# State-space scan: products with C one block behind the inputs, constants by transfers, first unit's inputs on VectorE

## The chip, the core and the metric

The program runs on one core of a Trainium2 chip. The time is the device time of one execution in microseconds (us), as a median over runs. The core has a matrix engine (TensorE, PE in the rows; PEld are its weight loads), a vector engine (VectorE, DVE), a scalar engine (ScalarE, ACT), a general engine (GpSimd, POOL) and a sync engine (SyncE, SP) that here only issues transfers. Each engine runs its own instructions in program order and they meet through semaphores.

## What is computed

x has 16 sequences of 512 rows of 256 numbers. It is normalised over its rows to xn; the result is x + A(xn) + F(xn). F is an attention layer and a mixture of experts. A is a state-space layer, and most of the change lies there:

```python
def step(state, inp):                       # for each of 512 time steps
    x_t, dt_t, B_t, C_t = inp
    dA = jnp.exp(jnp.clip(dt_t[:, :, None] * A[None], -10.0, 10.0))
    dB = dt_t[:, :, None] * B_t[:, None, :]
    state = jnp.clip(state * dA + x_t[:, :, None] * dB, -10.0, 10.0)
    y_t = jnp.einsum('bdn,bn->bd', state, C_t) + D * x_t
    return (state, y_t)
...
y = y * _silu(z)
return y @ W_out
```

There are 512 channels d, 16 state numbers n of each channel and 16 sequences b. dt is a softplus of a projection, x_in a SiLU of a convolution over time.

## The kernel before

Three stages run one after the other: build_attn (attention, the shared expert and the routing), build_experts, and build_mamba (the state-space layer with the final sum).

**The state-space stage** works in 32 chunks of 16 time steps. A chunk has four units u = 0 to 3: unit u is sub-chunk s = u // 2 (8 time steps) of half h = u % 2 (256 of the 512 channels, as two blocks i of 128). For each unit:

- POOL (inputs_of, L1530) writes the inputs B·dt·x of the unit into ub[:, h, i], one instruction of 128x2048 for each i, and counts u_ready.
- ACT (decays, L1640) writes the 32 decays exp(-A·dt), 32 instructions.
- DVE (scan, L1734 and L1742) makes 8 steps; a step is a product with the decay (L1734), the product with C of the step before (times_c, L1719), and the clipped sum with the input (L1742). The product with C goes into the same place of ub from which the input of that step was read. The last one of a unit is made in the first step of the next unit, and counts sc_unit.
- PE (nsum, L1884) sums the products over n with 32 matmuls, 16 for each i, and counts nsum_done after each 16.
- DVE (gate_y, L1753) multiplies the sum with the gate, in the seventh step of the next unit.

So ub has one buffer for each half: inputs, then products, then the next inputs of that half. inputs_of waits for nsum_done of the unit two back, for block i = 0 and then for block i = 1.

Between these, POOL makes in a fixed order for each chunk: gate_z of the next chunk (L1515, L1519), inputs of unit 2, dt_sum of the next chunk (L1496, L1502; the second waits for DVE's log_rest L1711, which is made in the first step of unit 2), inputs of unit 3, four gathers of expert rows (L1540), dt_times_x (L1509) of the next chunk, then the inputs of its units 0 and 1. All of it is in one queue. The loop over the chunks has two chunks in its body; the first and the last three stand outside.

SP issues the transfers of a chunk in order: store of the result of the chunk before (L1449), load of the residual (L1436), of the routes, store of B and C, and their loads broadcast over the partitions (L1429, L1431), with the load of rows (L1412) among them. Buffers xm, xn, res, ot, th_z, th_x, sp_u and sp_v each have memory of their own, and dtx has two.

**Ahead of the first chunk** POOL makes dt, dt·x and the inputs of units 0 and 1 in its queue, and DVE starts unit 0 when they are there.

**At the start of the kernel** DVE fills three rows of each of the two tiles kst with ones (L607), then takes the statistics of the first rows (L623, L631), scales w_q (L634) after all 17 weight loads (w_loaded), and makes a reciprocal (L637) on which ACT's first normalisation (L549) waits. ACT and PE each wait for all weight loads ahead of anything else.

## Time and profile before

| | |
|---|---|
| median of 3 runs | 4441.67 us (4422.38 to 4448.53) |
| the profiled execution | 4426.43 us, of which the span of the profile is 4424.3 us |
| state-space stage in the profile | from 2176 us to the end |
| busy, share of the span | PE 85%, DVE 67%, PEld 63%, ACT 57%, POOL 50% |
| busy tenths of DVE, in 40 slices | 4455455544545522222269999999999999999997 |
| busy tenths of POOL, in 40 slices | 2223333333333221000067777777777777777774 |

A slice is 110.6 us. The busy share says how full an engine is; whether it sets the time is seen from its waits. In the rows below a time is the start in us from the start of the span, the number behind it the duration in us, and what stands in brackets is how long the engine stood idle ahead of the instruction and what ended that.

### The profile page before, as it was taken

To read this page: it belongs to the slowest core of one execution; us is meant where nothing else is said; L and a number is where in the kernel's file an instruction comes from. 1 tells how busy PE (TensorE), PEld (TensorE's weight loads), DVE (VectorE), ACT (ScalarE), POOL (GpSimd) and SP (SyncE) were. 2 spreads that over 40 slices of the span, in tenths; PEclk is the share of its full clock that TensorE was granted. 3 is DMA by queue.
4 is the path that set the end of the run, shared out by engine and by line. 5 is a ranking of instruction groups with operands and counts; after the bars stand their busy time and mean duration, and the time that the engine had idled before them with its cause. 6 is when DMAs were issued, how large, how long until landed. Compare 5 with 4: busy or idle time off the path is not lost.

```text
span 4424.3 us, 70363 instructions
## 1 busy us (share of the span) xinstructions
PE 3743.7 (85%) x22136; PEld 2801.6 (63%) x22136; DVE 2973.9 (67%) x5485; ACT 2502.9 (57%) x6473; POOL 2202.6 (50%) x1120
## 2 busy tenths in 40 slices
PE   4888888888888875999869888889898998988886
PEld 2344444444444434777658888878787887888776
DVE  4455455544545522222269999999999999999997
ACT  1443343434433431333378777788778787777773
POOL 2223333333333221000067777777777787777774
PEclk8899999999999987999989999999999999999998
DMA  3322232223322214666522222222222222222221
GB/s 91 95 77 83 84 100 79 78 88 98 91 87 80 79 54 128 212 209 211 150 87 92 76 87 78 80 88 86 78 89 87 75 92 76 87 81 77 87 82 36
DMA packets 285737, 419.86 MB, mean 95 GB/s; under 512 B 77397, under 2 KB 249814, under 8 KB 262808
## 3 DMA queue, kind: packets, MB, share of 16 engines
q1 hardware_dynamic: 273048, 381.12, 26.6%
q0 software_dynamic: 12288, 33.57, 2.2%
q8 instruction: 230, 3.77, 0.4%
q14 instruction: 171, 1.40, 0.1%
HBM read 330.63 MB, written 83.17 MB: 94 GB/s over the span
## 4 chain that ended last, share of the span: by engine, by line
POOL 22%; issue 10%; PE 9%; DVE 8%; ACT 1%; DVEq 0%; POOLq 0%; DMA 0%; SPq 0%; ACTq 0%
POOL m_ub L1530 18%; PE m_Y L1884 7%; DVE m_PR L1734 2%; DVE m_S L1742 2%; DVE m_PR L1742 2%; DVE m_S L1734 1%; POOL m_th_z L1515 1%; POOL m_yg L1540 1%; DVE m_ub L1719 1%; ACT m_dA L1640 1%; POOL m_dtx L1509 1%; PE m_F L1846 1%; PE m_F L1895 0%; PE m_F L1820 0%; DVEq L1733 0%
## 5 line engine op out<-in xcount | busy, mean ns | idle before, releaser
L1530 POOL TENSOR_TENSOR m_ub<-m_Bb,m_dtx 128x2048 f32<-128x2048 f32 x256 | 1157.7, 4546 | 440.4 <-PE m_Y L1884 434.0
L1640 ACT ACTIVATE m_dA<-m_dt,m_a_neg 128x128 f32<-128x128 f32 x4096 | 1211.0, 387 | 168.8 <-DVE m_S L1742 167.6
L1884 PE MATMUL m_Y<-m_ub,m_ident 128*128 128x128 f32 x8192 | 1040.4, 293 | 204.6 <-DVE m_ub L1719 204.6
L1884 PEld LDWEIGHTS m_Y<-m_ub,m_ident 128*128 128x128 f32 x8192 | 1022.1, 208 | 218.4 <-DVE m_ub L1719 218.4
L539 ACT ACTIVATE f_pt<-f_X 128x512 f32<-128x512 f32 (+1 forms) x704 | 371.8, 554 | 712.9 <-PE f_X L841 691.2
L615 DVE TENSOR_REDUCE f_nm<-f_Y 128x1 f32<-128x512 f32 (+3 forms) x896 | 434.1, 530 | 354.4 <-PE f_Y L841 351.4
L1734 DVE SCALAR_TENSOR_TENSOR m_PR<-m_dA,m_S 128x512 f32<-128x512 f32 x512 | 355.6, 695 | 124.5 <-POOL m_ub L1530 53.8
L1734 DVE SCALAR_TENSOR_TENSOR m_S<-m_dA,m_PR 128x512 f32<-128x512 f32 x512 | 354.9, 693 | 12.0
L1742 DVE CUSTOM_DVE_ANT_1 m_PR<-m_PR,m_ub 128x512 f32<-128x512 f32 x512 | 353.2, 690 | 0.2 <-DVE m_PR L1734 0.2
L1742 DVE CUSTOM_DVE_ANT_1 m_S<-m_S,m_ub 128x512 f32<-128x512 f32 x512 | 353.2, 690 | 0.0
L1719 DVE TENSOR_TENSOR m_ub<-m_S,m_Cb 128x512 f32<-128x512 f32 x512 | 349.7, 683 | 0.0
L1719 DVE TENSOR_TENSOR m_ub<-m_PR,m_Cb 128x512 f32<-128x512 f32 x512 | 349.6, 683 | 0.0
L824 PE MATMUL f_Y<-f_kst,f_qst 96*128 96x512 bf16 (+3 forms) x1024 | 254.1, 328 | 107.2 <-DVE f_nm L615 89.7
L830 PE MATMUL f_X<-f_qst,f_kst 99*128 99x512 bf16 (+3 forms) x1024 | 263.0, 324 | 72.7 <-ACT f_pt L539 39.2
L489 POOL TENSOR_TENSOR f_kq<-f_ra,f_rb 128x512 f32<-128x512 f32 x64 | 80.7, 1268 | 459.6 <-DVE f_rb L643 442.6
L1178 DVE SCALAR_TENSOR_TENSOR e_sg<-e_th,e_G 128x512 f32<-128x512 f32 x70 | 48.1, 687 | 326.4 <-ACT e_th L1122 326.4
L1846 PE MATMUL m_F<-m_xpad,m_cv_diag 128*128 128x256 f32 x1024 | 260.3, 398 | 0.0
L824 PEld LDWEIGHTS f_Y<-f_kst,f_qst 96*128 96x128 bf16 x1024 | 84.8, 105 | 260.7 <-DVE f_nm L615 164.2
L1820 PE MATMUL m_F<-m_xnT,m_w_in 128*128 128x256 f32 x1024 | 235.8, 384 | 1.3 <-DMA m_w_in<-L_attn_W_in 1.3
L830 PEld LDWEIGHTS f_X<-f_qst,f_kst 99*128 99x128 bf16 x1024 | 91.5, 103 | 228.0 <-issue 129.4
L1483 POOL MEMSET m_ident<- 128x128 f32 x1 | 0.2, 204 | 470.7 <-POOLq L2012 470.7
L1846 PEld LDWEIGHTS m_F<-m_xpad,m_cv_diag 128*128 128x128 f32 x1024 | 187.2, 193 | 64.6 <-issue 43.6
(229 smaller groups left out, 6278.4 us busy)
## 6 DMA issues: line engine op xcount, KB each, us to landing
m_Bb<-m_bc_dram SPq DMA_DIRECT2D x64, 1024.0 KB, 4.6
m_Cb<-m_bc_dram SPq DMA_DIRECT2D x64, 1024.0 KB, 4.7
f_parts_dram<-f_parts SPq DMA_DIRECT2D x32, 768.0 KB, 4.1
f_kst<-f_parts_dram SPq DMA_DIRECT2D x192, 128.0 KB, 2.6
f_qst<-f_parts_dram SPq DMA_DIRECT2D x192, 128.0 KB, 2.6
e_rows<-sorted_rows SPq DMA_DIRECT2D x70, 256.0 KB, 2.7
e_wg<-Wg SPq DMA_DIRECT2D x70, 256.0 KB, 2.9
e_wu<-Wu SPq DMA_DIRECT2D x70, 256.0 KB, 3.9
```

Of the source, the lines that this page charges most:

```text
L539: act.activation(out, cols(bank_of(k, r)), func, **kw).then_inc(free_sem(k, r), 1)
L615: ins = dve.tensor_reduce(out, cols(full(k, r)), AX.X, ALU.max, negate=True)
L824: pe.matmul(bank[:, c0:c0 + n], qst[p][0:KS, h, qb * P:(qb + 1) * P], kst[p][0:KS, h, 0:n], start=(c0 == 0), stop=False, skip_group_check= ...
L830: pe.matmul(bank[:, c0:c0 + n], kst[p][:, h, kb * P:(kb + 1) * P], qst[p][:, h, kb * P:SEQ], start=(c0 == 0), stop=False, skip_group_check ...
L1530: pool.tensor_tensor(ub[:, h, i, :, :], Bb[:, s, :, :], dtx[:, par, m, None, s * SN:(s + 1) * SN].to_broadcast([P, NST, SN]), ALU.mult).th ...
L1640: last = act.activation(dA[:, h, i, n, :], dtt[:, par, m, s * SN:(s + 1) * SN], ACT.Exp, scale=a_neg[:, m, n:n + 1])
L1719: return dve.tensor_tensor(ub[:, h, :, :, cols], state[:, :].rearrange("p (i n b) -> p i n b", i=2, n=NST), Cb[:, s, None, :, cols].to_bro ...
L1734: dve.scalar_tensor_tensor(new, dA[:, h, :, :, cols].rearrange("p i n b -> p (i n) b"), DA_MIN, old, ALU.max, ALU.mult).then_inc(p_step, 1)
L1742: dve._custom_dve(bass.dve_ops.TENSOR_ADD_SAT, out=new, in0=new, in1=ub[:, h, :, :, cols].rearrange("p i n b -> p (i n) b"), s0=CLIP, s1=- ...
L1820: last = pe.matmul(F[(1 + i) % 4][:, m, :], w_in[:, k, blk * P:(blk + 1) * P], xnT[:, k, :], start=(k == 0), stop=(k == KM - 1))
L1846: last = pe.matmul(F[1 + i][:, j, :], cv_diag[:, k * MI + m, :], xpad[:, m, k * BATCH:k * BATCH + CN], start=False, stop=(k == TAPS - 1))
L1884: last = pe.matmul(Y[:, i * SN:(i + 1) * SN], ident[:, :], ub[:, h, i, n, :], start=False, stop=(n == NST - 1), skip_group_check=True)
```

## The change

In the state-space stage ub gets a third block for each half. The inputs are written into blocks 0 and 1, the products with C into blocks 1 and 2. The inputs of block 0 then wait only for the last step of the scan two units back (s_step); those of block 1 wait for the first 16 matmuls of the sum (nsum_done). dtx has one buffer in place of two, xn lies in xm, ot in res, sp_u in th_z and sp_v in th_x; with that go new waits (dt_ready ahead of ACT's tanh instructions, ot_stored ahead of the load of the residual, xT_done ahead of the load of rows). Ahead of the first chunk DVE makes dt, dt·x and the inputs of unit 0, POOL those of unit 1. At the start of the kernel the ones in kst come by six transfers from a tile of ones, issued by ACT, and ACT and PE wait for the weights only where they first use them.

```diff
@@ -430,6 +430,7 @@
         fixed(pool.memset(ident[:, :], 0.0))
         fixed(pool.affine_select(out=ident[:, :], in_=ident[:, :], compare_op=ALU.not_equal, fill=1.0,
                                  base=0, pattern=[[-1, P]], channel_multiplier=1))
+        fixed(pool.memset(onesb[:, :], 1.0))
         for q, value in enumerate((-0.5, 0.5, 1e-5, -1.0)):
             fixed(pool.memset(consts[:, q, :], value))
 
@@ -446,7 +447,6 @@
             fixed(pool.memset(before[:, :, :], 0.0))
             fixed(pool.affine_select(out=before[:, :, :], in_=before[:, :, :], compare_op=ALU.is_ge, fill=1.0,
                                      base=0, pattern=[[-1, ER], [1, ER]], channel_multiplier=0))
-            fixed(pool.memset(onesb[:, :], 1.0))
             fixed(pool.memset(tri[:, :], 0.0))
             fixed(pool.affine_select(out=tri[:, :], in_=tri[:, :], compare_op=ALU.is_ge, fill=1.0,
                                      base=0, pattern=[[-1, P]], channel_multiplier=1))
@@ -527,11 +527,15 @@
         run(nc.gpsimd, do)
         pool.wait_ge(scattered, 16 * TT * TOPK * BATCH)
 
-    N_CONST, N_CONST_FIRST = 26, 6
+    N_CONST, N_CONST_FIRST = 26, 7
 
     @block.scalar
     def _(act):
-        act.wait_ge(w_loaded, W_ALL)
+        act.wait_ge(const_ready, N_CONST_FIRST)
+        for p in range(2):
+            for q in range(PARTS):
+                act.dma_start(kst[p][KS + q:KS + q + 1, :, :].rearrange("a h t -> a (h t)").rearrange("a (p c) -> a p c", p=P),
+                              onesb[:, 0:NH * SEQ // P]).then_inc(q_scaled, 16)
 
         def reader(r):
             def read(k, out, cols, func, **kw):
@@ -562,6 +566,8 @@
                     last = act.activation(h2[:, t, :], x2[:, t, :], ACT.Copy, scale=sc2[:, 4, t:t + 1])
                 last.then_inc(h2_done, 1)
             if kind == "T":
+                if isinstance(b, int) and b == 0:
+                    act.wait_ge(w_loaded, W_ALL)
                 for k in range(KM):
                     read(("T", k), h1T[:, k, :], lambda bank: bank[:, :], ACT.Copy, scale=ln1[:, k:k + 1])
             if kind == "lat":
@@ -603,9 +609,6 @@
 
     @block.vector
     def _(dve):
-        for p in range(2):
-            dve.memset(kst[p][KS:KS + PARTS, :, :], 1.0).then_inc(q_scaled, 1)
-
         def full(k, r):
             dve.wait_ge(*filled(k, r))
             return bank_of(k, r)
@@ -758,7 +761,6 @@
 
     @block.tensor
     def _(pe):
-        pe.wait_ge(w_loaded, W_ALL)
         pe.wait_ge(const_ready, N_CONST_FIRST)
 
 
@@ -782,6 +784,8 @@
                 pe.wait_ge(h1_done, b + 1)
                 transposed("T", r, h1)
             if kind == "lat":
+                if isinstance(b, int) and b == 0:
+                    pe.wait_ge(w_loaded, W_ALL)
                 pe.wait_ge(*used(("T", 0), r))
                 pe.wait_ge(*used(("T", 1), r))
                 pe.sem_inc(taken)
@@ -791,7 +795,7 @@
                 full(("lat",), r, last)
             if kind == "kq":
                 if isinstance(b, int) and b == 0:
-                    pe.wait_ge(q_scaled, 3)
+                    pe.wait_ge(q_scaled, 1 + 16 * 2 * PARTS)
                 g, first, second = i, ("kq", i, j, 0), ("kq", i, j, 1)
                 if j == 0:
                     pe.wait_ge(*used(("lat",), r))
@@ -1273,7 +1277,7 @@
 
     xm = sb("m_xm", [P, TT, DM])
     rowsc = sb("m_rowsc", [P, TT, 2])
-    xn = sb("m_xn", [P, TT, DM])
+    xn = xm
     xnT = sb("m_xnT", [P, KM, CN])
     xpad = sb("m_xpad", [P, MI, HALO + CN])
     th_z = sb("m_th_z", [P, MI, CN])
@@ -1281,23 +1285,23 @@
     dt_in = sb("m_dt_in", [RANK + 1, CN])
     bc_row = sb("m_bc_row", [RANK + 2 * NST, CN])
     sp_e = sb("m_sp_e", [P, MI, CN])
-    sp_u = sb("m_sp_u", [P, MI, CN])
-    sp_v = sb("m_sp_v", [P, MI, CN])
+    sp_u = th_z
+    sp_v = th_x
     sp_r = sb("m_sp_r", [P, MI, CN])
     z_sb = sp_r
 
     x2 = sb("m_x2", [P, 2, MI, CN])
     zs = sb("m_zs", [P, 2, MI, CN])
     dtt = sb("m_dt", [P, 2, MI, CN])
-    dtx = sb("m_dtx", [P, 2, MI, CN])
+    dtx = sb("m_dtx", [P, MI, CN])
 
     dA = sb("m_dA", [P, 2, 2, NST, SN])
-    ub = sb("m_ub", [P, 2, 2, NST, SN])
+    ub = sb("m_ub", [P, 2, 3, NST, SN])
     Bb = sb("m_Bb", [P, NSUB, NST, SN])
     Cb = sb("m_Cb", [P, NSUB, NST, SN])
     yz = sb("m_yz", [P, MI, CN])
     res = sb("m_res", [P, TT, DM])
-    ot = sb("m_ot", [P, TT, DM])
+    ot = res
     info = sb("m_info", [P, 2, TT, 2 * TOPK])
     info_i = info[:, :, :, :].bitcast(mybir.dt.int32)
     yg = sb("m_yg", [P, TOPK, TT, DM])
@@ -1408,7 +1412,7 @@
 
         def load_x(c):
             rows = row_of(c)
-            held(xn_done, TT * c)
+            held(xT_done, c)
             sp.dma_start(xm[:, :, :], x_tm[bass.ds(rows, CN), :].rearrange("(j p) d -> p j d", p=P)).then_inc(x_loaded, 16)
             with nc.allow_non_contiguous_dma(reason="two numbers of a row"):
                 sp.dma_start(rowsc[:, :, :], stat_tm[bass.ds(rows, CN), :].rearrange("(j p) d -> p j d", p=P)).then_inc(x_loaded, 16)
@@ -1432,7 +1436,7 @@
 
         def load_res(c):
             rows = row_of(c)
-            held(ot_done, c)
+            held(ot_stored, 16 * c)
             sp.dma_start(res[:, :, :], res_tm[bass.ds(rows, CN), :].rearrange("(j p) d -> p j d", p=P)).then_inc(res_loaded, 16)
 
         def load_info(c, par):
@@ -1504,9 +1508,8 @@
         def dt_times_x(c, par):
             pool.wait_ge(dt_ready, c + 1)
             pool.wait_ge(x2_ready, 2 * (c + 1))
-            if not isinstance(c, int) or c >= 2:
-                pool.wait_ge(u_ready[NU - 1], 2 * (c - 1))
-            pool.tensor_tensor(dtx[:, par, :, :], x2[:, par, :, :], dtt[:, par, :, :], ALU.mult).then_inc(dtx_ready, 1)
+            pool.wait_ge(u_ready[NU - 1], 2 * c)
+            pool.tensor_tensor(dtx[:, :, :], x2[:, par, :, :], dtt[:, par, :, :], ALU.mult).then_inc(dtx_ready, 1)
 
         def gate_z(c, par):
 
@@ -1526,9 +1529,12 @@
             for i in range(2):
                 m = 2 * h + i
                 if not isinstance(pc, int) or pc >= 1:
-                    pool.wait_ge(nsum_done[pu], 2 * (pc - 1) + i + 1)
+                    if i == 0:
+                        pool.wait_ge(s_step, NU * ST * (pc - 1) + ST * (pu + 1) + 2)
+                    else:
+                        pool.wait_ge(nsum_done[pu], 2 * (pc - 1) + 1)
                 pool.tensor_tensor(ub[:, h, i, :, :], Bb[:, s, :, :],
-                                   dtx[:, par, m, None, s * SN:(s + 1) * SN].to_broadcast([P, NST, SN]),
+                                   dtx[:, m, None, s * SN:(s + 1) * SN].to_broadcast([P, NST, SN]),
                                    ALU.mult).then_inc(u_ready[u], 1)
 
         def gather(c, par):
@@ -1541,9 +1547,6 @@
                                             bass.IndirectOffsetOnAxis(ap=info_i[:, par, j, k:k + 1], axis=0)).then_inc(yg_loaded, 16)
 
         gate_z(0, 0)
-        dt_sum(0, 0)
-        dt_times_x(0, 0)
-        inputs_of(0, 0, 0)
         inputs_of(0, 0, 1)
 
         def body(c, par, first, last):
@@ -1591,6 +1594,7 @@
                 act.activation(xpad[:, 2 * hx:2 * hx + 2, HALO:HALO + CN], F[1 + hx][:, :, :], ACT.Copy).then_inc(xpad_ready, 1)
                 act.wait_ge(xz_done, 4 * c + 2 * i + 2)
                 act.wait_ge(zs_ready, c)
+                act.wait_ge(dt_ready, c)
                 act.activation(th_z[:, 2 * i:2 * i + 2, :], F[(3 + i) % 4][:, :, :], ACT.Tanh, scale=0.5).then_inc(thz_ready, 1)
                 act.wait_ge(sp_sub, c)
                 act.activation(z_sb[:, 2 * i:2 * i + 2, :], F[(3 + i) % 4][:, :, :], ACT.Copy).then_inc(z_copied, 1)
@@ -1600,6 +1604,7 @@
                 hx = 1 - i
                 act.wait_ge(conv_done, 2 * c + i + 1)
                 act.wait_ge(x2_ready, 2 * c)
+                act.wait_ge(dt_ready, c)
                 act.activation(th_x[:, 2 * hx:2 * hx + 2, :], F[1 + hx][:, :, :], ACT.Tanh, scale=0.5).then_inc(thx_ready, 1)
 
         def evac_dbc(c):
@@ -1716,7 +1721,7 @@
             s, h = u // 2, u % 2
             cols = slice(t * BATCH, (t + 1) * BATCH)
             state = (S[h], PR)[(t + 1) % 2]
-            return dve.tensor_tensor(ub[:, h, :, :, cols], state[:, :].rearrange("p (i n b) -> p i n b", i=2, n=NST),
+            return dve.tensor_tensor(ub[:, h, 1:3, :, cols], state[:, :].rearrange("p (i n b) -> p i n b", i=2, n=NST),
                                      Cb[:, s, None, :, cols].to_broadcast([P, 2, NST, BATCH]), ALU.mult)
 
         def scan(c, u, between, before_it):
@@ -1740,7 +1745,7 @@
                 dve.wait_ge(p_step, base + t + 1)
                 dve.sem_inc(taken)
                 dve._custom_dve(bass.dve_ops.TENSOR_ADD_SAT, out=new, in0=new,
-                                in1=ub[:, h, :, :, cols].rearrange("p i n b -> p (i n) b"),
+                                in1=ub[:, h, 0:2, :, cols].rearrange("p i n b -> p (i n) b"),
                                 s0=CLIP, s1=-CLIP).then_inc(s_step, 1)
                 if t in between:
                     between[t]()
@@ -1778,6 +1783,20 @@
         dve.tensor_scalar(a_neg[:, :, :], a_neg[:, :, :], -1.0, None, ALU.mult).then_inc(setup_neg, 1)
         silu_x(0, 0)
         log_rest(0)
+        dve.wait_ge(sp_ln, 1)
+        dve.wait_ge(sp_relu, 2)
+        dve.tensor_tensor(sp_u[:, :, :], sp_u[:, :, :], sp_r[:, :, :], ALU.add).then_inc(sp_sub, 1)
+        dve.wait_ge(sp_sub, 1)
+        dve.wait_ge(sp_low, 1)
+        dve.tensor_tensor(dtt[:, 0, :, :], sp_u[:, :, :], sp_v[:, :, :], ALU.subtract).then_inc(dt_ready, 1)
+        dve.wait_ge(dt_ready, 1)
+        dve.wait_ge(x2_ready, 2)
+        dve.tensor_tensor(dtx[:, :, :], x2[:, 0, :, :], dtt[:, 0, :, :], ALU.mult).then_inc(dtx_ready, 1)
+        dve.wait_ge(dtx_ready, 1)
+        dve.wait_ge(b_loaded[0], 16)
+        for i in range(2):
+            dve.tensor_tensor(ub[:, 0, i, :, :], Bb[:, 0, :, :], dtx[:, i, None, 0:SN].to_broadcast([P, NST, SN]),
+                              ALU.mult).then_inc(u_ready[0], 1)
 
         def body(c, par, first, last):
             slots = [dict() for _ in range(NU)]
@@ -1881,7 +1900,7 @@
             pe.wait_ge(sc_unit[u], c + 1)
             for i in range(2):
                 for n in range(NST):
-                    last = pe.matmul(Y[:, i * SN:(i + 1) * SN], ident[:, :], ub[:, h, i, n, :], start=False, stop=(n == NST - 1),
+                    last = pe.matmul(Y[:, i * SN:(i + 1) * SN], ident[:, :], ub[:, h, 1 + i, n, :], start=False, stop=(n == NST - 1),
                                      skip_group_check=True)
                 last.then_inc(nsum_done[u], 1)
 
```

## Rows read from the trace of the kernel before

**Rows 1.** Groups of VectorE, 2311 to 4200 us: busy us, mean ns | idle before, releasers.

```profile
L1734 DVE SCALAR_TENSOR_TENSOR m_PR<-m_dA,m_S 128x512 f32<-128x512 f32 x447 | 310.4, 695 | 82.2 <-issue 30.2 <-DVE m_S L1742 28.3 <-POOL m_ub L1530 13.7
...
L1753 DVE TENSOR_TENSOR m_yz<-m_Y,m_zs 128x256 f32<-128x256 f32 x112 | 46.2, 413 | 0.0
```

**Rows 2.** Timeline of VectorE, first steps of units following each other.

```profile
3117.84 0.70 DVE L1734 SCALAR_TENSOR_TENSOR m_PR<-m_dA,m_S 128x512 f32<-128x512 f32 x1 [2.49 <-issue]
...
3134.40 0.70 DVE L1734 SCALAR_TENSOR_TENSOR m_PR<-m_dA,m_S 128x512 f32<-128x512 f32 x1
...
3151.35 0.70 DVE L1734 SCALAR_TENSOR_TENSOR m_PR<-m_dA,m_S 128x512 f32<-128x512 f32 x1 [0.89 <-DVE m_S L1742]
...
3168.04 0.70 DVE L1734 SCALAR_TENSOR_TENSOR m_PR<-m_dA,m_S 128x512 f32<-128x512 f32 x1
...
3184.14 0.69 DVE L1734 SCALAR_TENSOR_TENSOR m_PR<-m_dA,m_S 128x512 f32<-128x512 f32 x1 [0.51 <-POOL m_ub L1530]
```

**Rows 3.** Timeline of GpSimd in the same chunk.

```profile
3124.82 9.04 POOL L1530 TENSOR_TENSOR m_ub<-m_Bb,m_dtx 128x2048 f32<-128x2048 f32 x2 [9.16 <-PE m_Y L1884]
...
3142.11 9.05 POOL L1530 TENSOR_TENSOR m_ub<-m_Bb,m_dtx 128x2048 f32<-128x2048 f32 x2 [3.39 <-PE m_Y L1884]
...
3154.56 2.36 POOL L1502 TENSOR_TENSOR m_dt<-m_sp_u,m_sp_v 128x1024 f32<-128x1024 f32 x1 [1.08 <-issue]
...
3158.33 9.05 POOL L1530 TENSOR_TENSOR m_ub<-m_Bb,m_dtx 128x2048 f32<-128x2048 f32 x2 [1.41 <-PE m_Y L1884]
...
3167.53 0.99 POOL L1540 DMA_INDIRECT m_yg<-expert_rows,m_info  x1
...
3174.90 9.03 POOL L1530 TENSOR_TENSOR m_ub<-m_Bb,m_dtx 128x2048 f32<-128x2048 f32 x2 [0.22 <-POOL m_dtx L1509]
```

**Rows 4.** Timeline of TensorE in the same chunk.

```profile
3119.19 9.04 PE L1884 MATMUL m_Y<-m_ub,m_ident 128*128 128x128 f32 x64 [4.06 <-DVE m_ub L1719]
...
3152.69 9.04 PE L1884 MATMUL m_Y<-m_ub,m_ident 128*128 128x128 f32 x64 [3.18 <-DVE m_ub L1719]
```

**Rows 5.** Timeline ahead of the first chunk, ScalarE and GpSimd.

```profile
2219.14 1.28 ACT L1640 ACT_TABLE_LOAD   x1 [4.92 <-POOL m_dt L1502]
...
2220.43 18.81 ACT L1640 ACTIVATE m_dA<-m_dt,m_a_neg 128x128 f32<-128x128 f32 x64
...
2221.56 17.95 POOL L1530 TENSOR_TENSOR m_ub<-m_Bb,m_dtx 128x2048 f32<-128x2048 f32 x4
```

**Rows 6.** Timeline of VectorE in the first chunk.

```profile
2230.64 0.70 DVE L1734 SCALAR_TENSOR_TENSOR m_PR<-m_dA,m_S 128x512 f32<-128x512 f32 x1 [17.91 <-POOL m_ub L1530]
...
2272.37 1.29 DVE L1711 SCALAR_TENSOR_TENSOR m_sp_v<-m_F,m_sp_e 128x512 f32<-128x512 f32 x2 [2.35 <-ACT m_F L1623]
...
2309.62 0.70 DVE L1734 SCALAR_TENSOR_TENSOR m_PR<-m_dA,m_S 128x512 f32<-128x512 f32 x1 [3.89 <-POOL m_ub L1530]
```

**Rows 7.** Timeline of GpSimd at the end of the loop.

```profile
4189.11 0.95 POOL L1540 DMA_INDIRECT m_yg<-expert_rows,m_info  x1 [5.68 <-issue]
```

**Rows 8.** Timeline of VectorE at the end of the loop.

```profile
4204.27 0.69 DVE L1734 SCALAR_TENSOR_TENSOR m_PR<-m_dA,m_S 128x512 f32<-128x512 f32 x1 [5.71 <-POOL m_ub L1530]
```

**Rows 9.** Groups of VectorE, 4205 us to the end.

```profile
L1734 DVE SCALAR_TENSOR_TENSOR m_PR<-m_dA,m_S 128x512 f32<-128x512 f32 x47 | 32.6, 695 | 8.9 <-POOL m_ub L1530 7.3
```

**Rows 10.** Timeline of VectorE at the start of the kernel.

```profile
11.06 6.88 DVE L607 MEMSET f_kst<- 3x8192 bf16 x1 [1.66 <-issue]
...
23.33 0.18 DVE L637 RECIPROCAL f_sc<-f_sc 128x4 f32<-128x4 f32 x1 [3.16 <-POOL f_sc L473]
```

**Rows 11.** Transfers, 0 to 60 us: busy tenths in 40 slices; packets, MB, engine share.

```profile
DMA  0599879998000000000000000000000000680675
...
q1 hardware_dynamic: 5513, 5.00, 28.6%
```

**Rows 12.** Timeline in the attention stage, VectorE and GpSimd.

```profile
769.18 0.22 DVE L722 TENSOR_TENSOR f_picked<-f_oh,f_wt 128x56 f32<-128x56 f32 x1
...
781.34 1.09 DVE L734 TENSOR_TENSOR f_picked<-f_oh,f_slot 128x56 f32<-128x56 f32 x1
...
781.09 1.27 POOL L489 TENSOR_TENSOR f_kq<-f_ra,f_rb 128x512 f32<-128x512 f32 x1 [2.20 <-DVE f_rb L643]
```

## The prediction

> **What bounds the kernel now.** The slices of the page say that VectorE is nine tenths busy from the second fifth of the state-space stage to its end, and no other engine is; so the question for that stage is what VectorE's remaining idle time waits for. I read the groups of VectorE first. In the loop over the chunks all idle time of note stands ahead of L1734, the first step of a unit [rows 1]: 30.2 us under "issue", 28.3 us under "DVE m_S L1742" and 13.7 us under "POOL m_ub". The first is the jump back at the end of the loop body, one of about 2.3 us in each two chunks, as in the 2.49 us of [rows 2]; nothing in the change touches it. The second is named after VectorE itself, but that engine had long been done. The timeline shows who it was: the inputs that begin at 3142.11 end at 3151.16, and unit 2 starts at 3151.35; those that begin at 3174.90 end at 3183.93, and the next chunk starts at 3184.14 [rows 2, 3]. Both labels are therefore one wait, for GpSimd's inputs, and together 42.0 us.
>
> Why GpSimd is late is read from its own idle time: 9.16, 3.39 and 1.41 us ahead of its inputs, each ended by TensorE's sum L1884 [rows 3]. GpSimd may write over a buffer only after TensorE has summed the products in it, and both blocks (9.05 us) stand behind that. The cycle is: last product, 16 matmuls, two input instructions, next unit of that half.
>
> **Part 1: a third block (loop).** After the change the input of block 0 needs only the end of the scan two units back, that of block 1 the first half of the sum. I set the chunk of [rows 2 to 4] again, with U0 to U3 as the starts of its units. VectorE's own work takes 16.5 us for unit 0 (3117.84 to 3134.4), 16.7 for unit 2 and 15.6 for unit 3 [rows 2], 16.05 for unit 1.
> - Unit 2: block 0 can be written from U0 + 16.6 to 21.1. The half sum is there at 3142.11, U0 + 24.3, so block 1 is ready at U0 + 28.8, where unit 2 is due at U0 + 32.55. It was ready at 33.3. The 0.9 us go, with 3.7 us to spare.
> - Unit 1: the half sum is there at 3124.82, U0 + 7.0; block 1 is ready at U0 + 11.5, due at 16.5.
> - Unit 3: dt ends at 3156.92, U2 + 5.6 [rows 3], and it isn't moved, since it hangs on VectorE's log_rest in unit 2. Then 9.05 us of inputs with no wait between them: 3152.69 starts the sum, 3158.33 has half of it [rows 3, 4], and block 1 needs it only at U2 + 10.1. Ready at U2 + 14.6, due at U2 + 16.7.
> - Unit 0 of the next chunk: four gathers and dt·x take 3167.53 to 3174.90, 7.4 us, then 9.03 us [rows 3]. From U2 + 14.8 that ends at U2 + 31.2; due at U2 + 16.7 + 15.6 = 32.3. This is the tightest place, with 1.1 us to spare.
>
> So all waits for inputs in the loop fall away, **42.0 us**. What is late next is nothing within a unit: VectorE is then bound by its own steps and the jumps. GpSimd's reordered instructions are the same ones at the same price; it runs beside the same steps as before, only earlier.
>
> **Part 2: the end of the loop and the last chunks.** At the loop's end one gather is held up by 5.68 us [rows 7], on no semaphore that the profile shows, and VectorE waits 5.71 us at 4204.27 [rows 8]. That delay stays. The inputs of unit 3 end 1.3 us earlier there (by the same sum: from dt without the 1.4 us wait for TensorE), so **1.3 us**; with luck up to 3.4, what is left above a jump of 2.3. Behind that, 7.3 us of waits for inputs [rows 9] go as in the loop: **7.3 us**. The very end (last sum, gate, projection) isn't touched.
>
> **Part 3: ahead of the first chunk.** VectorE's 256-wide product takes 413 ns and a 512-wide one about 695 [rows 1], so some 1.1 ns an element: an estimate of 1.27 us for 1024 elements and 2.4 for 2048. GpSimd's two instructions for dt kept ScalarE waiting 4.92 us [rows 5]; two of VectorE take 2.6 with the hops between. dt is ready 2.2 us earlier, at about 2216.9. dt·x (1.3) and two inputs (4.8) would be done at about 2223, but the decays of unit 0 take a table load of 1.28 and half of 18.81 us [rows 5]: 2227.6. So unit 0 starts 3.0 us earlier than at 2230.64 [rows 6], not 7. In its first chunk VectorE then waits for ScalarE at log_rest (2272.37, [rows 6]), which moves by the 2.2 us of dt only; the waits ahead of it melt into that one. From there 2.2 us remain, and the 3.89 us ahead of the next chunk [rows 6] go as in the loop: **6.1 us**.
>
> VectorE's new instructions have both operands in SBUF, and GpSimd's inputs of unit 1 start on the same signal. The trace shows what that does: a small product of two such operands takes 0.22 us alone, but 1.09 us where it starts at 781.34 beside a GpSimd instruction that ends at 782.36; it ends as that one does [rows 12]. So VectorE's inputs may stand behind GpSimd's, 4.5 + 2.4 + 4.5 + 2.4 us from 2218.2, and unit 0 starts at 2232 in place of 2227.6. The wait at log_rest hides this too, so the 6.1 us stand; were that cover gone, it would cost 4.4 us. The Trainium skill says in "SBUF — State Buffer", section "Who interferes with whom", that a DVE instruction with two SBUF inputs contends with a GpSimd instruction that reads SBUF, and that whoever issues first holds the shared ports for all of it. By that rule, the trace agrees for the first unit; and in the loop each instruction of VectorE has one operand in PSUM, so the rule has nothing to take there. If it did bind in the loop, the gain of part 1 would be in doubt; it is what speaks most against moving work between these two engines.
>
> **Part 4: the start of the kernel.** Two fills of 6.88 us stand ahead of the statistics on VectorE; the second ends at 17.9, and the reciprocal on which all waits runs at 23.33 [rows 10]. Without them it waits for the weights, since the scaling of w_q stands ahead of it. All transfers are over by the tenth slice of 1.5 us, 15.0 us [rows 11]; with their signal and the scaling the reciprocal could run at about 15.9. The six transfers of ones add 768 short packets. From 28.6% of 16 engines over 60 us for 5513 packets [rows 11], a packet costs 50 ns of one engine, so 768 cost 2.4 us over 16 engines if all were full, nothing if they fit in gaps. The reciprocal comes at 15.9 to 18.3; I take 17.1, **6.2 us** less (5.0 to 7.4). The work of the attention stage follows from that instruction in a chain, so it moves as a whole. ScalarE issues the six ahead of its first normalisation, by about 6 us, long before it is due; TensorE's wait for the ones lies at its first kq, past 25 us.
>
> **Part 5: shared memory and new waits**, all costed at nothing.
> - ScalarE waits for dt_ready ahead of the tanh of z. dt is ready at U2 + 5.6; ScalarE gets there after the decays of unit 3, 9.4 us and a table load into unit 2, at about U2 + 11.5. Behind it in its queue are the decays of the next chunk, which wait for U3 anyway. Cover: 5.9 us.
> - SP waits for the result to be stored before it loads the residual, some 3 us longer. Behind it stand the routes and the loads of B and C. The load of C waits for unit 1 anyhow, and B is wanted at U2 + 22, some 20 us later than it lands.
> - dtx with one buffer: dt·x already stands behind the inputs of unit 3 in GpSimd's queue. The load of rows waits for a transpose made a unit before.
>
> **The sum**: 42.0 + 1.3 + 7.3 + 6.1 + 6.2 = 62.9 us. The profiled execution took 4426.43 us, so 4363.5. The median of the runs shown is 15 us above that execution; taken off it, 4441.67 - 62.9 = **4378.8 us**.
>
> **The rivals.**
> - *The slack isn't there* (18%). The tightest place has 1.1 us in 66, worked out from one chunk, and GpSimd's spans are rough. If the chain from dt over the gathers to the next inputs is longer by that, half of the 49.3 us stays as waits: 62.9 - 24.7 = 38.2 us, 4403.5. For it: GpSimd still has some 53 us of work in 66. Against: its durations hardly vary.
> - *TensorE takes over* (8%). It is the busiest engine over the span, 85%. If its sums set the starts, through the gate or the blocks of ub, none of parts 1 and 2 is had: 12.3 us, 4429.4. Against: it waits 4.06 and 3.18 us for VectorE at its sums [rows 4], so it follows VectorE and not the other way round.
> - *Slower* (4%): dt_ready comes late. The tanh of z now waits for dt, which stands in GpSimd's queue behind the inputs of unit 2 and behind VectorE's log_rest. If GpSimd makes dt more than 5.9 us later than now, ScalarE stands; it hurts VectorE only once the decays of the next chunk come late too, which take 9.4 of the 15.6 us of unit 3, so from 5.9 + 6.2, some 12 us later than now. Each us beyond costs 31 us in 31 chunks; 3 us beyond would give 4441.7 - 62.9 + 93 = 4472.
>
> **Chances.** The forecast 70%, the rivals 18, 8 and 4%. About 0.5% (22 us) is what a measurement of this kernel can tell from no change. Faster: 70 + 18 = 0.88; same: 0.08; slower: 0.04. The range takes in the forecast's own spread and the first rival. Low: 4360, from the sum off the profiled time and 3 us more of bounds (2.1 at the loop's end, 1.2 at the start). High: 4406, the first rival with the start's bound.
>
> **What the profile would show.** Ahead of L1734 the labels "DVE m_S" and "POOL m_ub" shrink to near nothing in the loop, "issue" stays at 30 us. GpSimd's two inputs of a unit stand apart, the first right after a unit's end, the second behind L1884. The first unit starts at 2228 or 2232 less the 6 us of the start, the reciprocal near 17. Wrong would be: POOL waits that stay ahead of unit 0 (the slack), waits of the gate L1753 for TensorE, or decays L1640 that end late.

## The result, and the profile after

| | median | runs |
|---|---|---|
| kernel before | 4443.73 us | 4 runs, 4422.38 to 4448.53 |
| changed kernel | 4381.06 us | 4 runs, 4378.37 to 4389.52 |

The ratio is 0.9881 with a 95% interval of 0.9853 to 0.9909: 53 us less, between 40 and 65. The medians of the table are 62.7 us apart, and in a second set of runs (below) the changed kernel took 4394.23 us beside 4437.29 for before, 43.1 apart, ratio 0.9894. The forecast was 4378.8 us. That closeness is partly luck: the saving worked out was 62.9 us, counted from waits in the profiled execution of before. The profiled execution of the changed kernel took 4378.37 us with a span of 4376.6, so between the two profiles only **47.7 us** went, and the rest came from a median of before that lies above its profiled execution. It is the 47.7 that have to be accounted for.

The page of the changed kernel, busy time of TensorE and VectorE's tenths in 40 slices:

```profile
PE 3733.1 (85%) x22136; PEld 2784.6 (64%) x22136; DVE 2974.2 (68%) x5488; ACT 2499.8 (57%) x6473; POOL 2194.1 (50%) x1115
...
DVE  3455455544545432222279999999999999999998
```

VectorE is nine tenths busy to the end of the state-space stage, as before. Its groups in the loop (2299 to 4160 us), first step of the pair and first clipped sum:

```profile
L1739 DVE SCALAR_TENSOR_TENSOR m_PR<-m_dA,m_S 128x512 f32<-128x512 f32 x447 | 310.4, 694 | 42.4 <-issue 30.5
...
L1747 DVE CUSTOM_DVE_ANT_1 m_PR<-m_PR,m_ub 128x512 f32<-128x512 f32 x448 | 309.3, 690 | 10.0 <-issue 10.0
```

The first row answers [rows 1]: 82.2 us have become 42.4, "DVE m_S" and "POOL m_ub" are no longer among its releasers, and "issue" stands at 30.5. The second row is new: 10.0 us of "issue" ahead of a clipped sum, which had none before. The timeline of VectorE over one pair of chunks shows where:

```profile
3095.62 0.70 DVE L1739 SCALAR_TENSOR_TENSOR m_PR<-m_dA,m_S 128x512 f32<-128x512 f32 x1 [2.31 <-issue]
...
3096.22 0.68 DVE L1724 TENSOR_TENSOR m_ub<-m_S,m_Cb 128x512 f32<-128x512 f32 x1
...
3097.58 0.70 DVE L1747 CUSTOM_DVE_ANT_1 m_PR<-m_PR,m_ub 128x512 f32<-128x512 f32 x1 [0.68 <-issue]
...
3112.94 0.69 DVE L1739 SCALAR_TENSOR_TENSOR m_PR<-m_dA,m_S 128x512 f32<-128x512 f32 x1
...
3129.03 0.69 DVE L1739 SCALAR_TENSOR_TENSOR m_PR<-m_dA,m_S 128x512 f32<-128x512 f32 x1
...
3145.72 0.70 DVE L1739 SCALAR_TENSOR_TENSOR m_PR<-m_dA,m_S 128x512 f32<-128x512 f32 x1
...
3161.35 0.70 DVE L1739 SCALAR_TENSOR_TENSOR m_PR<-m_dA,m_S 128x512 f32<-128x512 f32 x1
```

The units at 3112.94, 3129.03, 3145.72 and 3161.35 start with no wait. The jump is there as before (2.31), and two instructions behind it the clipped sum waits another 0.68 us for nothing that the profile names. GpSimd in the same chunk:

```profile
3112.99 4.55 POOL L1536 TENSOR_TENSOR m_ub<-m_Bb,m_dtx 128x2048 f32<-128x2048 f32 x1 [1.25 <-DVE m_S L1747]
...
3120.70 4.55 POOL L1536 TENSOR_TENSOR m_ub<-m_Bb,m_dtx 128x2048 f32<-128x2048 f32 x1 [3.15 <-PE m_Y L1903]
...
3134.58 9.08 POOL L1536 TENSOR_TENSOR m_ub<-m_Bb,m_dtx 128x2048 f32<-128x2048 f32 x2
...
3151.19 9.05 POOL L1536 TENSOR_TENSOR m_ub<-m_Bb,m_dtx 128x2048 f32<-128x2048 f32 x2 [0.24 <-POOL m_dtx L1512]
```

These rows answer [rows 3]. For unit 2 the two blocks stand apart: the first at 3112.99, right after a scan's end (3112.94 is the next unit's first step), the second at 3120.70 behind TensorE's sum. Unit 3's 9.08 us stand together with no wait. The next chunk's, at the place that had 1.1 us to spare on paper, end at 3160.24, and VectorE starts at 3161.35: 1.1 us.

To see where the 47.7 us lie, I cut each span at fixed instructions: the end of attention (VectorE's first instruction of the expert stage), the start of the state-space stage (GpSimd's first m_ident), the first step of chunks 0, 1 and 29, and the end.

| us | before | after | less | forecast |
|---|---|---|---|---|
| attention stage | 1705.0 | 1702.4 | 2.6 | 6.2 |
| expert stage | 470.7 | 467.9 | 2.8 | 0 |
| state space, up to the first unit | 55.0 | 51.9 | 3.1 | 3.0 |
| chunk 0 | 79.0 | 75.3 | 3.7 | 3.1 |
| loop, chunk 1 to chunk 29, with its end | 1894.7 | 1864.7 | 30.0 | 43.3 |
| last chunks and end | 220.0 | 214.4 | 5.6 | 7.3 |

### The profile page after: what moved, and what is told of

The parts are those of the page before. It is cut to its first block, busy times and chain, and to the rows that moved or that the text cites. A ratio compares the mean times of both kernels' runs of the same rounds, so it can differ in the third digit from the quotient of the medians.

```text
span 4376.6 us, 70452 instructions
## 1 busy us (share of the span) xinstructions
PE 3733.1 (85%) x22136; PEld 2784.6 (64%) x22136; DVE 2974.2 (68%) x5488; ACT 2499.8 (57%) x6473; POOL 2194.1 (50%) x1115
## 4 chain that ended last, share of the span: by engine, by line
DVE 35%; issue 11%; PE 2%; ACT 1%; DVEq 1%; POOL 0%; DMA 0%; SPq 0%; POOLq 0%; ACTq 0%
DVE m_S L1747 8%; DVE m_PR L1747 8%; DVE m_S L1739 7%; DVE m_PR L1739 7%; DVE m_ub L1724 1%; DVE m_yz L1758 1%; ACT m_dA L1645 1%; DVE m_x L1708 1%; DVE m_th_x L1716 1%; DVEq L1738 1%; PE m_F L1865 1%; DVE m_res L1766 0%; PE m_Y L1903 0%; POOL m_ub L1536 0%; PE m_F L1839 0%
## 5 line engine op out<-in xcount | busy, mean ns | idle before, releaser
L1903 PE MATMUL m_Y<-m_ub,m_ident 128*128 128x128 f32 x8192 | 1024.9, 290 | 161.4 <-DVE m_ub L1724 161.4
L1903 PEld LDWEIGHTS m_Y<-m_ub,m_ident 128*128 128x128 f32 x8192 | 1007.3, 206 | 174.2 <-DVE m_ub L1724 174.2
L1739 DVE SCALAR_TENSOR_TENSOR m_PR<-m_dA,m_S 128x512 f32<-128x512 f32 x512 | 355.5, 694 | 53.6 <-issue 30.5
L1487 POOL MEMSET m_ident<- 128x128 f32 x1 | 0.2, 205 | 467.9 <-POOLq L2031 467.9
L1865 PEld LDWEIGHTS m_F<-m_xpad,m_cv_diag 128*128 128x128 f32 x1024 | 186.5, 192 | 63.9 <-issue 43.1
```

The source lines that it names most:

```text
L1739: dve.scalar_tensor_tensor(new, dA[:, h, :, :, cols].rearrange("p i n b -> p (i n) b"), DA_MIN, old, ALU.max, ALU.mult).then_inc(p_step, 1)
L1865: last = pe.matmul(F[1 + i][:, j, :], cv_diag[:, k * MI + m, :], xpad[:, m, k * BATCH:k * BATCH + CN], start=False, stop=(k == TAPS - 1))
L1903: last = pe.matmul(Y[:, i * SN:(i + 1) * SN], ident[:, :], ub[:, h, 1 + i, n, :], start=False, stop=(n == NST - 1), skip_group_check=True)
```

## The experiments

The state-space stage is the sharper measure: its length repeats within 1 to 3 us for the same kernel (2206.3 in the profile of the changed kernel, 2209.3 in another, below). The 3 us lie in chunk 0, which took 75.3 us in the one and 78.4 in the other. There TensorE's convolution products took nearly twice as long for a while (the second group of them, after and then the other profile), and VectorE waited 2.54 us for TensorE's sum at a gate where it had waited 0.46, and 0.86 for ScalarE behind it:

```profile
2237.55 1.99 PE L1865 MATMUL m_F<-m_xpad,m_cv_diag 128*128 128x256 f32 x8
```

```profile
2253.95 3.78 PE L1865 MATMUL m_F<-m_xpad,m_cv_diag 128*128 128x256 f32 x8
```

The granted clock over chunk 0 is 0.81 in the one and 0.78 in the other. The loop repeats within 1 us (1864.7 and 1865.5). The attention stage does not repeat: nearly the same instructions took 1697 to 1739 us in the profiles of this study, so each comparison below is by stage where the trace allows it. The next three kernels ran on one chip, beside runs of before with a median of 4431.38 us.

**Each part alone: the start.** The changed kernel with the old start: the two fills on VectorE, and the early waits for the weights.

```diff
-                act.dma_start(kst[p][KS + q:KS + q + 1, :, :]..., onesb[:, 0:NH * SEQ // P]).then_inc(q_scaled, 16)
+        act.wait_ge(w_loaded, W_ALL)
...
+            dve.memset(kst[p][KS:KS + PARTS, :, :], 1.0).then_inc(q_scaled, 1)
...
+        pe.wait_ge(w_loaded, W_ALL)
```

> The changed kernel with only the start of the kernel as it was before: ones in kst by two fills on VectorE, ScalarE and TensorE wait for all weights first. My theory: the new start is worth the 2.5 us by which the attention stage ends earlier in the profile of the changed kernel (2.6 us at the first product with the rope table), not the 4.8 us of the reciprocal and not the 6.2 forecast, because TensorE runs the first products at the lower clock after it. So 2 to 3 us slower than the changed kernel, some 50 us faster than the kernel before. Rival: the 2.8 us by which the experts' stage came out shorter belong to it too; then 5 us slower. On the gap of 0.76 us behind the jump of the loop: if it comes from where the loop lies in VectorE's instructions, it may change here, since two fills are added ahead.

Median 4390.0 us (4 runs, 4376.75 to 4419.12), ratio to before 0.989 (0.9862 to 0.9918). The runs spread over 42 us and can't tell 2 us from 5. The profile can: reciprocal at 23.34, first product of the rotation (L645 after) at 40.85 us, where the changed kernel has it at 35.59. Over the profiles of this study, nine with the new start have it at 33.4 to 36.2, mean 34.6; three with the old one have it at 38.2, 38.2 and 40.85, mean 39.1. The start is worth some 4.5 to 4.8 us, not 6.2. The new start, ScalarE's queue and VectorE:

```profile
2.42 4.04 ACTq L537 DMA_DIRECT2D f_kst<-f_onesb  x6
...
4.77 1.40 DVE L626 BATCH_NORM_STATS2 f_st<-f_xm 128x6 f32<-128x256 f32 x4 [4.77 <-DMA f_xm<-x_tm]
...
18.10 0.42 DVE L637 TENSOR_SCALAR f_w_q<-f_w_q 64x512 f32<-64x512 f32 x1 [11.60 <-DMA f_ln<-w_ln]
...
18.56 0.18 DVE L640 RECIPROCAL f_sc<-f_sc 128x4 f32<-128x4 f32 x1
...
35.59 0.69 DVE L645 TENSOR_TENSOR f_ra<-f_Z,f_rope 128x512 f32<-128x512 f32 x1 [16.85 <-PE f_Z L807]
```

The reciprocal is at 18.56 and not at 17.1: the scaling ahead of it waits for the last of the weights to 18.10. That load's signal came at 15.9 in before (issued at 10.15, landed 5.7 us later) and at 18.1 here (issued at 11.51, landed 6.6 us later), although the six transfers carry 16 KB each. Behind the reciprocal the two profiles differ too. From TensorE's first transpose to that product it is 12.7 us after and 10.1 before, since two of the three groups of products between them took nearly twice as long. After, then before:

```profile
25.83 3.75 PE L794 MATMUL f_Z<-f_h1T,f_w_lat 128*128 128x512 f32 x4 [0.98 <-ACT f_h1T L543]
...
30.32 2.04 PE L805 MATMUL f_Z<-f_lat,f_w_q 64*128 64x512 f32 x2 [0.73 <-issue]
...
32.29 3.26 PE L807 MATMUL f_Z<-f_h1T,f_w_kra 128*128 128x512 f32 x4
```

```profile
30.89 3.52 PE L790 MATMUL f_Z<-f_h1T,f_w_lat 128*128 128x512 f32 x4 [0.82 <-ACT f_h1T L539]
...
35.15 1.09 PE L801 MATMUL f_Z<-f_lat,f_w_q 64*128 64x512 f32 x2 [0.73 <-issue]
...
36.17 1.98 PE L803 MATMUL f_Z<-f_h1T,f_w_kra 128*128 128x512 f32 x4
```

That is TensorE's clock, and not the new start's doing. The view of the clock reads 1.00 in these stretches only because the trace has no record there: the first one, at the full level, stands at 34.9 us in this profile of the changed kernel and at 34.1 in that of before. In every profile of the study a product of 512 columns takes 1.06 us ahead of that first record and 0.59 us behind it, so it marks the rise. The rise came 12 to 15 us after TensorE's first instruction in some executions and 6 to 7 in others. With it the time from the reciprocal to the product L645 is 17.0 to 17.6 us or 14.6 to 14.9, under either start: long in this kernel and in four of the nine with the new start, the changed kernel's profile among them; short in the other five, in before and in the kernel before with twelve counts (below). So the lower clock that was put down above is there, but it doesn't take back what the new start gains: the two profiles under Result happened to be one of each kind.

**Each part alone: the first unit.** dt, dt·x and the inputs of the first unit back on GpSimd, with the third block and the new start kept.

```diff
+        dt_sum(0, 0)
+        dt_times_x(0, 0)
+        inputs_of(0, 0, 0)
         inputs_of(0, 0, 1)
...
-        dve.tensor_tensor(sp_u[:, :, :], sp_u[:, :, :], sp_r[:, :, :], ALU.add).then_inc(sp_sub, 1)
...
-            dve.tensor_tensor(ub[:, 0, i, :, :], Bb[:, 0, :, :], dtx[:, i, None, 0:SN].to_broadcast([P, NST, SN]),
```

> The changed kernel with dt, dt*x and the inputs of unit 0 of the first chunk on GpSimd again. My theory: unit 0 starts 3 us later against the start of the stage, and 2.2 us of that last to the next chunk; so 2 to 3 us slower than the changed kernel. Rival A (ports shared by VectorE and GpSimd): VectorE's two-operand products stood behind GpSimd's in the changed kernel, so putting them back costs under 1 us. Rival B: the 0.76 us at the first clipped sum behind each jump (10 us in 13 jumps) comes from the dozen instructions that stand ahead of VectorE's loop; without them the gap goes, and this kernel is 7 us faster than the changed one.

Median 4382.47 us (4371.72 to 4389.04), ratio 0.9878 (0.9849 to 0.9907). By stages the first unit comes 2.3 us later than in the changed kernel (54.2 us into the stage against 51.9), chunk 1 only 1.0 us later (128.2 against 127.2), and yet the state-space stage is **10.3 us shorter** (2196.0): the loop takes 1854.0 where the changed kernel takes 1864.7. Its groups, in the loop:

```profile
L1742 DVE SCALAR_TENSOR_TENSOR m_PR<-m_dA,m_S 128x512 f32<-128x512 f32 x447 | 310.4, 694 | 42.4 <-issue 30.5
...
L1750 DVE CUSTOM_DVE_ANT_1 m_PR<-m_PR,m_ub 128x512 f32<-128x512 f32 x448 | 309.1, 690 | 0.0
```

The 10.0 us ahead of the clipped sum are gone, with an identical loop: the lines are three further down, and the instructions and their waits are the same. Only what stands ahead of the loop in VectorE's queue differs. So the work moved to VectorE brings 2.3 us at the first unit, of which 1.0 is left at chunk 1, and costs 10 in the loop. Rival B was right. In the changed kernel the inputs themselves show the two engines in each other's way. VectorE, then GpSimd:

```profile
2212.62 8.81 DVE L1798 TENSOR_TENSOR m_ub<-m_Bb,m_dtx 128x2048 f32<-128x2048 f32 x2
...
2222.20 0.70 DVE L1739 SCALAR_TENSOR_TENSOR m_PR<-m_dA,m_S 128x512 f32<-128x512 f32 x1 [0.77 <-ACT m_dA L1645]
...
2263.53 1.29 DVE L1716 SCALAR_TENSOR_TENSOR m_th_x<-m_F,m_sp_e 128x512 f32<-128x512 f32 x2 [6.00 <-ACT m_F L1628]
...
2212.67 13.14 POOL L1536 TENSOR_TENSOR m_ub<-m_Bb,m_dtx 128x2048 f32<-128x2048 f32 x2 [19.74 <-DVE m_dtx L1794]
```

VectorE's two inputs take 8.81 us, where two alone would take 4.8 by the estimate of part 3, and GpSimd's two take 13.14 in place of 9.04 [rows 3]. Both start at 2212.6 and take turns, VectorE first: the four instructions end at 2214.91, 2219.28, 2221.43 and 2225.81, VectorE's and GpSimd's in turn. [rows 12] had shown the like for a small one. The prediction had priced GpSimd's going first, which would have put VectorE's second input 4.5 us later. The Trainium skill says in "SBUF — State Buffer", section "Who interferes with whom", that a VectorE instruction with two SBUF inputs contends with a GpSimd instruction that reads SBUF; by that rule, the trace agrees. It cost nothing here: unit 0 waits 0.77 us for the decays at the end, and what is left melts into the wait of 6.00 us at 2263.53 for ScalarE (2.35 in [rows 6]), as the sum had it.

**The earlier waits, taken away.** Both blocks wait for the sum as before, in the changed kernel; the third block's memory stays.

```diff
-                    if i == 0:
-                        pool.wait_ge(s_step, NU * ST * (pc - 1) + ST * (pu + 1) + 2)
-                    else:
-                        pool.wait_ge(nsum_done[pu], 2 * (pc - 1) + 1)
+                    pool.wait_ge(nsum_done[pu], 2 * (pc - 1) + i + 1)
```

> The changed kernel, three blocks and shared buffers kept, but the input of block 0 waits for TensorE's sum as in the kernel before. My theory: the earlier start of block 0 is the whole gain in the state-space stage; the waits ahead of L1739 come back in the loop (some 40 us) and behind it (5 to 7 us), so 40 to 47 us slower than the changed kernel, and within 12 us of the kernel before. Rival: part of the gain comes from the shared buffers or from the earlier first unit, which shift the engines against each other; then less than 30 us slower than the changed kernel.

Median 4436.21 us (10 runs), ratio to before 1.001 (0.9991 to 1.003): with the old waits put back (block 0 for the first half of the sum, block 1 for the second) nothing is left of the whole change that these runs can tell. The state-space stage takes 2262.4 us, 56.1 more than in the changed kernel: 46.5 more in the loop, 5.5 behind it, 4 ahead of it. The group of the first steps in the loop, over the same steps as [rows 1]:

```profile
L1736 DVE SCALAR_TENSOR_TENSOR m_PR<-m_dA,m_S 128x512 f32<-128x512 f32 x447 | 310.3, 694 | 88.1 <-DVE m_S L1744 34.9 <-issue 30.4 <-POOL m_ub L1533 12.8
```

The waits for GpSimd are 47.7 us against 42.0 in [rows 1], and "issue" is as it was. What makes the 5.7 us more was not tried; the waits on the sum are before's word for word, so it lies in something else that the change brought. The gap behind the jump (9.2 us here) is still in it, so the loop is 16.5 us longer than before's. That the earlier start of the inputs is the gain in the loop is shown; how much of it is block 0's wait and how much block 1's was not tried apart.

**Where the slack ends.** The first rival rested on 1.1 us of slack. Two kernels put a piece of dt·x once more into GpSimd's queue, ahead of the product in dt_times_x: one block of four (0.8 us in a chunk) or all four (2.5 us, 2.6 in what was expected), each with a wait for it.

```diff
+            pool.tensor_tensor(dtx[:, 0:1, :], x2[:, par, 0:1, :], dtt[:, par, 0:1, :], ALU.mult).then_inc(filled_up, 1)
+            pool.wait_ge(filled_up, c)
```

> The changed kernel with one more product of 256 numbers on GpSimd in each chunk, ahead of dt*x (about 0.8 us with its hop), in the chain from dt over the gathers to the inputs of the next chunk. My theory: the chain has 1.1 us to spare (in the profile of the changed kernel the inputs end at 3160.24 and the next chunk starts at 3161.35), so the state-space stage keeps its 2206 us within 3. Rival: GpSimd already sets the start of unit 0; then 0.8 us a chunk, 25 us more.

> As the one with 256 numbers, but 1024 (a second dt*x, 2.4 us and 0.2 of hop). My theory: 2.6 us less the 1.1 to spare is 1.5 us in each chunk whose end isn't a jump of the loop, and less where a jump gives 2.3 us more: some 25 to 30 us more in the state-space stage (2232 to 2236), as waits ahead of unit 0 for GpSimd. Rival A: GpSimd sets the pace, 2.6 us in each chunk, 80 us. Rival B: TensorE sets it, under 10 us.

Each was executed once: 4396.23 and 4414.64 us, beside 4446.21 for before. With 0.8 us the state-space stage took 2207.0 us and the loop 1865.0, as without it. With 2.5 us they took 2232.5 and 1887.3, 22.6 us more in the loop. Its group over the loop, then a first step behind a jump and the next one with no jump ahead:

```profile
L1742 DVE SCALAR_TENSOR_TENSOR m_PR<-m_dA,m_S 128x512 f32<-128x512 f32 x447 | 310.4, 694 | 62.8 <-POOL m_ub L1539 46.6 <-issue 4.8
```

```profile
3116.54 0.70 DVE L1742 SCALAR_TENSOR_TENSOR m_PR<-m_dA,m_S 128x512 f32<-128x512 f32 x1 [2.38 <-issue]
...
3183.93 0.70 DVE L1742 SCALAR_TENSOR_TENSOR m_PR<-m_dA,m_S 128x512 f32<-128x512 f32 x1 [1.55 <-POOL m_ub L1539]
```

A chunk that begins behind a jump waits some 2.3 us as ever; most of these now stand under GpSimd's name and not under "issue", since the late inputs fall within the jump. What is new is the 1.5 us at each of the 14 chunks of the loop that begin without a jump: the idle time ahead of the first steps is 20.4 us more (62.8 against 42.4), and the wait at the loop's end 2.5 more. So 2.5 us on GpSimd came through as 1.5: the slack is there, some 1.0 us, and the 1.1 us fit.

**The gap behind the jump.** Two explanations stood: the new kernel's loop holds something that stalls the clipped sum, or the place of the loop in VectorE's instruction stream does it. The second can be moved without touching the loop: instructions that only count a semaphore, ahead of it. Twelve of them in the kernel **before**, and 32 in the changed kernel:

```diff
+        for _ in range(12):          # 32 in the changed kernel
+            dve.sem_inc(taken)
         silu_x(0, 0)
```

> The kernel before with twelve instructions that only count a semaphore on VectorE, ahead of its loop over the chunks; nothing else. Theory of place: the gap of 0.76 us at the first clipped sum behind each jump in the changed kernel comes from where the loop lies in VectorE's instructions, since eleven more (thirteen instructions with waits, less two fills) stand ahead of it. Then the gap shows here too, 0.7 to 1.1 us in each of 13 jumps, and the loop gets some 10 us longer, or less where a wait for inputs swallows it. Rival: the gap belongs to the three blocks or the shared buffers; then none here, and the stage keeps its 2249 us.

> The changed kernel with 32 instructions that only count a semaphore on VectorE ahead of its loop. Theory of place: the gap of 0.76 us behind each jump is a matter of where the loop starts, so it moves or goes; if it goes, the state-space stage takes 10 us less, near 2196 us as in the run with the first unit on GpSimd. Rival: the first unit on VectorE causes it in another way; then the gap stays and the stage takes 2206 us.

Each was executed once. The kernel before with twelve counts took 4464.01 us (beside 4446.21 without them), and its state-space stage was 21.2 us longer (2269.9; the loop 1913.6, 18.9 more). The jump itself has doubled: the last sum of the body ends at 3143.97, and the next step follows 4.33 us later.

```profile
3143.28 0.69 DVE L1742 CUSTOM_DVE_ANT_1 m_S<-m_S,m_ub 128x512 f32<-128x512 f32 x1
...
3148.30 0.70 DVE L1734 SCALAR_TENSOR_TENSOR m_PR<-m_dA,m_S 128x512 f32<-128x512 f32 x1 [4.33 <-issue]
```

Over the loop "issue" is 57.1 us in place of 30.2, and the waits for inputs went down from 42.0 to 33.6, since GpSimd works on through the longer jump. The gap at the clipped sum that was expected did not show: at its new place this loop pays at the jump itself. In the changed kernel 32 counts took the gap away: stage 2194.1, loop 1853.4. This one execution took 4360.59 us, 17.8 less than the profiled one of the changed kernel; 5.2 us of that are the attention stage.

To see what that is worth in runs, the changed kernel and the one with the counts ran again on one chip, beside before at 4437.29 us.

> The changed kernel again, beside the three that follow. My theory: the state-space stage takes 2206 us within 2 in every execution; what differs between executions of one kernel is the attention stage (1697 to 1739 us from profile to profile so far, with TensorE's mean clock from 0.923 to 0.936). So the profile shows 2204 to 2208 us in that stage, and the median lies 45 to 60 us under the kernel before. Rival: the state-space stage itself varies by 10 us, and the gains read from single profiles aren't what the change is worth.

> The changed kernel with 32 instructions on VectorE ahead of the loop that only count a semaphore. My theory: the loop loses the gap behind each jump, 11 to 12 us, in every execution; median 8 to 14 us below that of the changed kernel. Rival: the one profile was a lucky one; within 4 us of the changed kernel.

The changed kernel: 4394.23 us (4382.79 to 4397.28), ratio 0.9894 (0.9859 to 0.993), stage 2209.3, loop 1865.5. With the counts: 4381.2 us (4372.85 to 4384.51), ratio 0.9867 (0.9833 to 0.9901), stage 2196.1, loop 1853.5. By stages it is 12 to 13 us, twice; the medians differ by 13.0 and their ranges overlap. VectorE behind a jump, with the counts:

```profile
3109.54 0.70 DVE L1739 SCALAR_TENSOR_TENSOR m_PR<-m_dA,m_S 128x512 f32<-128x512 f32 x1 [2.26 <-issue]
...
3110.14 0.68 DVE L1724 TENSOR_TENSOR m_ub<-m_S,m_Cb 128x512 f32<-128x512 f32 x1
...
3110.75 0.69 DVE L1747 CUSTOM_DVE_ANT_1 m_PR<-m_PR,m_ub 128x512 f32<-128x512 f32 x1
```

The jump takes 2.26 us as ever, and the clipped sum at 3110.75 follows at once. The other kernels agree: those that have the changed kernel's instructions ahead of the loop all have the gap, whatever GpSimd does beside it (9.2 us with the wait for the sum, 9.6 and 9.8 with the two fillers), and the one with the old start, two instructions further on, has 12.2. Why the place matters, and at which places it does, isn't settled: three positions are known with no gap (before, the first unit on GpSimd, 32 counts), two with one, and one with a doubled jump.

**A still earlier start.** If the reciprocal waits for weights that it doesn't need, the wait can be taken from it. The column loads go first, under a signal of their own, and the scaling of w_q goes behind the first reciprocal; the 32 counts are kept.

```diff
+            sp.dma_start(ln1[:, :], w_ln1.rearrange("(k p) -> p k", p=P)).then_inc(lns_loaded, 16)
...
-                    act.wait_ge(w_loaded, W_ALL)
+                    act.wait_ge(lns_loaded, 32)
...
+                if isinstance(b, int) and b == 0:
+                    dve.wait_ge(w_loaded, W_ALL)
+                    dve.tensor_scalar(w_q[LAT:P, :, :, :], w_q[LAT:P, :, :, :], 1.0 / math.sqrt(HD), None, ALU.mult).then_inc(q_scaled, 1)
```

> The 32 instructions, and the start of the kernel once more: the two small column loads go first and have a semaphore of their own, VectorE scales w_q after the first reciprocal, so that only TensorE's first product with a weight waits for the 15 weight loads. My theory: the reciprocal runs near 10 us in place of 18.6, the transposes follow, and the latent product starts when the weights are there, near 17 us in place of 25.8; the first product with the rope table at 26 to 29 us (33.4 to 36.1 so far), so the attention stage starts 7 us earlier. Rival: TensorE's clock takes most of it back, as with the first step of this kind (4.8 us at the reciprocal, some 2.6 to 4.4 left at the rope product); then 3 us or less.

The chain at the start, VectorE and then TensorE:

```profile
9.83 0.18 DVE L638 RECIPROCAL f_sc<-f_sc 128x4 f32<-128x4 f32 x1 [3.46 <-POOL f_sc L474]
...
28.08 0.69 DVE L646 TENSOR_TENSOR f_ra<-f_Z,f_rope 128x512 f32<-128x512 f32 x1 [9.35 <-PE f_Z L808]
...
14.46 1.94 PE L779 MATMUL f_Z<-f_ident,f_h 128*128 128x128 f32 x8 [14.46 <-POOL f_run L455]
...
18.42 3.75 PE L795 MATMUL f_Z<-f_h1T,f_w_lat 128*128 128x512 f32 x4 [2.02 <-DMA f_wd<-Wd]
...
22.91 2.04 PE L806 MATMUL f_Z<-f_lat,f_w_q 64*128 64x512 f32 x2 [0.73 <-issue]
```

The reciprocal is at 9.83 us. Of the 8.7 us gained there some 7 are left at the product L646 (28.08 here, 26.12 in the last kernel below, against a mean of 34.6), as TensorE's first product waits at 18.42 for the weights after all. Median 4372.19 us (4365.52 to 4379.06), ratio 0.9856 (0.982 to 0.9892). The ranges of this kernel and of the one with the counts alone (4372.85 to 4384.51) overlap, so in runs the second new start isn't told apart.

**Fewer jumps.** Four chunks in a loop body, so 6 jumps back in place of 13; with the 32 counts.

```diff
-            with eng.Fori(0, NCH // 2 - 2) as g:
-                body(g * 2 + 1, 1, False, False)
-                body(g * 2 + 2, 0, False, False)
+            with eng.Fori(0, (NCH - 4) // 4) as g:
+                body(g * 4 + 1, 1, False, False)
...
+                body(g * 4 + 4, 0, False, False)
```

> The 32 instructions, and four chunks in the body of the loop in place of two, on every engine. My theory: 6 jumps of VectorE in place of 13, each 2.3 us, so 16 us less in the loop (1837 from 1853), if the longer body brings no stalls of its own. Rival: the longer body must be fetched in pieces and stalls in its middle, on VectorE or on TensorE with some 1300 instructions in it; then the gain is under 5 us, or a loss.

Median 4363.14 us (4351.83 to 4368.1), ratio 0.9831 (0.9794 to 0.9869). The loop takes 1837.5 us, 16.0 less than with two chunks in a body; "issue" ahead of the first steps is 14.0 us in place of 30. Seven jumps at 2.3 us are 16.1. The jump's price is shown by this, and the longer body brings no stall of its own.

**All together.** The start, the counts and four chunks in a body.

> The 32 instructions, four chunks in the loop body and the second new start in one kernel. My theory: the parts lie in different stages and add up: state-space stage 2180 to 2184 us, the first rope product near 28 us; median 5 to 9 us below the kernel with four chunks and the 32 instructions alone, some 78 us below the kernel before. Rival: the new start's gain is lost in the attention stage, whose length differs by up to 40 us between executions; then it can't be told from that kernel.

Median 4356.2 us (6 runs, 4340.14 to 4364.23), beside before at 4430.13 on that chip: ratio 0.982 (0.9789 to 0.985), state-space stage 2178.6 us. It is the fastest kernel of this study, 74 us under before; by the ratios (0.982 against 0.9881 and 0.9894) it is some 27 to 33 us under the changed kernel.

**The attention stage.** What makes its length vary isn't settled. Stretch, length, busy time of PE, PEld, DVE, ACT and POOL with instructions, then the granted clock, the DMA share and GB/s, for 60 to 1700 us; the kernel before, the changed one, the one with the old start, and the one with 32 counts:

```profile
60.00:1700.00 1640.00, 1358.49 (x7720) 696.92 (x7720) 786.90 (x1919) 641.64 (x1189) 520.58 (x510) 0.91 0.27 83
```

```profile
60.00:1700.00 1640.00, 1363.30 (x7720) 697.05 (x7720) 787.23 (x1919) 640.79 (x1189) 520.58 (x510) 0.91 0.27 83
```

```profile
60.00:1700.00 1640.00, 1374.23 (x7659) 703.65 (x7659) 778.06 (x1890) 638.27 (x1180) 512.12 (x499) 0.89 0.27 83
```

```profile
60.00:1700.00 1640.00, 1356.62 (x7718) 690.74 (x7716) 790.12 (x1928) 640.72 (x1189) 523.25 (x524) 0.91 0.27 83
```

The work is the same, its matmuls longer or shorter in sum (1356.6 to 1374.2 us for nearly as many), and the granted clock is 0.89 in the longest of the four and 0.91 in the others. The profile with the old start had 1738.6 us in that stage, the one with 32 counts 1697.2, and neither kernel changes anything there beyond the first 40 us. The profile of before ran with the same clock as that of after, so this doesn't explain the missing gain; but it is why I read the start's worth at the product L645 and not at the end of the stage.

## Why the prediction was right, and where it was off

**Right:** the reading of two labels as one wait. With the earlier waits both are gone in the loop, and putting the old ones back costs 46.5 us there. The other ways that I had named did not come: the slack of 1.1 us is measured as 1.0 (0.8 us more on GpSimd costs nothing, 2.5 come through as 1.5 a chunk), VectorE waits for TensorE nowhere in the loop, and no wait for dt_ready shows up. The last chunks gained 5.6 us (forecast 7.3), the end of the loop waits 4.34 us in place of 5.71 [rows 8], 1.4 against a forecast of 1.3:

```profile
4162.25 0.70 DVE L1739 SCALAR_TENSOR_TENSOR m_PR<-m_dA,m_S 128x512 f32<-128x512 f32 x1 [4.34 <-POOL m_ub L1536]
```

**Right, but in part not told apart:** part 3. The first unit came 3.1 us earlier (3.0), the two engines took turns, and the wait for ScalarE at log_rest covered it. The first chunk's share in all was 6.8 us (6.1) in this profile, but 4.1 in the second one of the same kernel (chunk 0 took 78.4 us in place of 75.3). And of the 6.8 us, 5.8 were there with the first unit's inputs on GpSimd too, where the sum had given the blocks 3.9: for the move itself, priced at 2.2 by chunk 1, 1.0 is left, less than chunk 0 varies by.

**Off, part 1.** "42.0 us" was the sum of the waits, and "nothing in the change touches it" was said of the jump. The waits did go, and the idle time ahead of the first steps fell by 39.8 us; a wait that goes still leaves the ordinary 0.03 us between two units. Then the sentence on the jump failed: the change puts ten-odd instructions ahead of the loop in VectorE's queue, and with the loop at that place each jump is followed by another 0.7 us at the clipped sum, 10.0 us in all. The loop with its end gave 30.0 us in place of 43.3. That the place does it is shown from three sides: fewer instructions ahead (10.7 us back in the loop), 32 more (11.3 and 12.0 back), and the kernel before with twelve more (18.9 us lost, though at the jump itself and not at the clipped sum). I had priced part 3 by the time of its instructions and its ports, and had no term for what an instruction ahead of a loop does to the loop.

**Off, part 4.** The term was 6.2 us (5.0 to 7.4); the reciprocal came 4.8 us earlier, at 18.56 where 15.9 to 18.3 was forecast and 17.1 taken. Two sizes of the sum were off. The six transfers had been costed by their packets at 0 to 2.4 us and taken at 1.2; the signal of the last weights came 2.2 us later, at 18.1 against 15.9. And 0.9 us had been allowed for that signal and the scaling behind the last transfer at 15.0; they take 1.3, since the signal alone comes at 15.9. The chain behind moves as forecast, but has one of two lengths, some 2.5 us apart, by when TensorE's clock rises, whichever the start: the profile of before had the short one, that of the changed kernel the long one, and so only 2.6 us show in the table.

**What was not foreseen at all** is the expert stage, 2.8 us shorter with no change in it; over the profiles it lies between 467.5 and 473.4 us, so that is its spread.

The sum of these: 39.8 - 10.0 + 1.4 is 31.2 us for the loop and its end by idle time; by the cut it is 30.0, since VectorE's own steps took 1.3 us more in all (1797.5 against 1796.2). With 6.8 for the first chunk, 5.6 for the last, 2.6 and 2.8 ahead of the stage it is 47.7 us, but for rounding. The medians are 62.7 us apart all the same, because before's stands 17.3 us over its profiled execution and after's 2.7: those 14.6 us stood in for the 15.2 that the sum had too much. That the forecast time came out within 2.3 us of the median is luck; that the saving was forecast with the right mechanism, and too large by a quarter of itself, is not.

## What to carry to other kernels

Follow a wait to the engine that was really late, and give its cycle one more buffer only where a dependence other than the last one can release it: here the next inputs need the scan's end, not the sum of all its products, and taking that away again cost 46 us in the loop. Before work is moved onto the engine that bounds a loop, count what stands ahead of the loop in its queue, and compare "issue" at and behind the jump by groups before and after; a few counting instructions more or fewer can be worth 10 to 20 us. Compare by stages with fixed instructions as cuts, where one stage of the program varies more than the change is worth.

## What the runs showed of the hardware

- A jump back of a loop costs VectorE about 2.3 us in all kernels but one, 4.3 in that one; six jumps in place of thirteen gave 16.0 us. With identical instructions in the loop, the place of the loop in the instruction stream decided over 0, 0.7 to 1.1, or 2 us more for each jump.
- Two queues of large instructions with both operands in SBUF, VectorE's and GpSimd's, took turns instruction by instruction: 8.81 us for VectorE's two, 13.14 for GpSimd's two, from the same start.
- Six transfers of 16 KB in short packets beside the weight loads went with a last weight's signal at 18.1 us in place of 15.9 (16.3 and 16.5 in the two other profiles without them).
- TensorE's first products run at the lower clock: 1.06 us for a product of 512 columns ahead of the trace's first record of the clock, 0.59 us behind it, in all 14 profiles. The rise came 5.9 to 14.7 us after TensorE's first instruction, with identical instructions up to there 6.5 us in one execution of the changed kernel and 12.0 in another, which moves the chain at the start by some 2.5 us.
- Later on too the clock makes the spread: chunk 0 of the changed kernel took 75.3 us at a granted clock of 0.81 and 78.4 at 0.78.
